# First layer's cross attention: one TensorE step interleaves both passes, GpSimd splits the maxima, and the second pass runs fifteen steps behind the first

## The reference, cut to what matters

```python
# q = x, k = v = ctx_2048, each (32, 64, 256); 8 heads split the 64 rows of a sequence
qk = jnp.einsum('bhdq,bhdl->bhql', qh, kh) * scale      # dq = 8, Lq = Lk = 256
sm = jax.nn.softmax(qk, axis=-1)
ret = jnp.einsum('bhql,bhdl->bhdq', sm, vh)
x = _layernorm(x + gamma * ret)
```

## Time and profile before

| | us |
|---|---|
| median of 3 runs | 1250.38 (1249.96 to 1255.8) |
| profiled execution | 1244.66 |
| its span in the trace | 1242.6 |
| cross attention within the span, about | 163 to 428 |
| PE, DVE, ACT, POOL busy in the span | 1103.5, 800.7, 585.0, 454.7 |
| DMA, sums and products (line 779), issue to landing, the page's median | 3.0 |

### The profile page before, as it was taken

How to read it: one execution, slowest core, us unless ns; L and a number is a source line. 1 busy time by engine, 2 the same in 40 slices (tenths; PEclk the granted TensorE clock), 3 DMA queues, 4 the chain that set the end, 5 groups by cost and what they waited for, 6 DMA issues and landing times. The chain is left out here.

```text
span 1242.6 us, 20732 instructions
## 1 busy us (share of the span) xinstructions
PE 1103.5 (89%) x7356; PEld 652.4 (53%) x7356; DVE 800.7 (64%) x1547; ACT 585.0 (47%) x1209; POOL 454.7 (37%) x692
## 2 busy tenths in 40 slices
PE   6888769998998599999878999869997999999997
PEld 3566535454554245777433555647775343545455
DVE  4899886888886142333576668647885456465555
ACT  2666506766767331343376555348773422121110
POOL 6999851555534245333235346431111000000001
PEclk9999978999999799999999999989997999999999
DMA  6964354655662112453503000020000000000000
GB/s 219 309 192 143 94 131 106 147 139 142 149 143 73 47 56 97 125 170 120 174 1 135 1 1 1 1 69 2 2 2 5 21 1 0 9 9 9 8 9 26
DMA packets 75354, 95.90 MB, mean 77 GB/s; under 512 B 12883, under 2 KB 62189, under 8 KB 74573
## 3 DMA queue, kind: packets, MB, share of 16 engines
q1 hardware_dynamic: 70835, 84.92, 24.1%
q0 software_dynamic: 3408, 9.34, 2.1%
q10 hardware_dynamic: 1010, 0.31, 0.1%
HBM read 57.47 MB, written 31.27 MB: 71 GB/s over the span
## 5 line engine op out<-in xcount | busy, mean ns | idle before, releaser
L918 ACT ACTIVATE a_late<-a_qkv 128x512 f32<-128x512 f32 x128 | 77.3, 604 | 59.3 <-PE a_qkv L995 59.3
L2654 POOL TENSOR_SCALAR f_rstd<-f_mv 128x1 f32<-128x1 f32 x16 | 3.8, 239 | 266.5 <-DVE f_mv L2793 266.4
L866 DVE TENSOR_REDUCE b_nm<-a_s 128x4 f32<-128x1024 f32 x64 | 78.0, 1219 | 30.8 <-PE a_s L964 30.8
L2738 DVE TENSOR_TENSOR f_prod<-f_sg,f_kept 128x512 f32<-128x512 f32 (+1 forms) x48 | 33.2, 692 | 96.4 <-ACT f_kept L2683 93.5
L2863 PE MATMUL fps_h<-residT,w_f_w 128*128 128x512 f32 x176 | 82.4, 608 | 2.5 <-DVE f_inner L2775 2.5
L866 DVE TENSOR_REDUCE b_nm<-a_pt 128x4 f32<-128x1024 f32 x64 | 76.7, 1199 | 2.3 <-PE a_pt L964 2.3
L918 ACT ACTIVATE a_late<-a_y 128x512 f32<-128x512 f32 x128 | 77.0, 602 | 0.0
L2677 ACT ACTIVATE f_sg<-fps_h 128x512 f32<-128x512 f32 (+1 forms) x24 | 14.3, 596 | 125.2 <-PE fps_h L2882 108.3
L1010 PE MATMUL a_o<-a_late,b_vt 128*32 128x256 f32 x1024 | 69.2, 389 | 0.0
L1320 POOL DMA_INDIRECT routed<-c_out,c_target x39 | 37.4, 959 | 67.2 <-ACT c_out L1401 66.9
L1974 DVE SCALAR_TENSOR_TENSOR d_acc<-d_pad,d_cw,d_acc 128x512 f32<-128x512 f32 x72 | 58.4, 815 | 4.9 <-ACT d_acc L1880 3.2
(11 more groups left out here) (428 smaller groups left out, 2896.9 us busy)
## 6 DMA issues: line engine op xcount, KB each, us to landing
kparts<-a_rest SPq DMA_DIRECT2D x48, 192.0 KB, 3.8
a_rest<-a_rest SPq DMA_DIRECT2D x64, 128.0 KB, 3.0
xrows<-in_c_fill SPq DMA_DIRECT2D x13, 387.0 KB, 4.5
c_xrow<-xrows SPq DMA_DIRECT2D x39, 129.0 KB, 2.1
c_back<-routed SPq DMA_DIRECT2D x16, 256.0 KB, 3.6
a_front<-kparts SPq DMA_DIRECT2D x12, 288.0 KB
a_front<-qparts SPq DMA_DIRECT2D x36, 96.0 KB
qparts<-b_xp SPq DMA_DIRECT2D x48, 64.0 KB, 2.8
```

The lines of the kernel that those rows point to most:

```text
L866: dve.tensor_reduce(nm[s % 2][:, 4 * n:4 * n + 4].rearrange("p (g h) -> p g h", h=2), s1[step % 2][:], AX.X, ALU.max, negate=True).then_in ...
L918: act.activation(pr[g % 8][:], s2[g % 2][:], ACT.Exp, scale=SCALE).then_inc(s2_out, 1)
L2738: dve.tensor_tensor(prod[n % 2][at], sg[n % 2][at], up, ALU.mult).then_inc(prod_done, 1)
```

## The change

Five things are changed, all in `cross_attention`.

1. PE's step is written in another order. Before: first pass (4 matmuls), both heads of the second pass (2 + 2), and in every other step all 8 value matmuls. Now: half of the values (4 matmuls, one `lh`) in every step, second pass of head 2j, first pass, second pass of head 2j + 1.
2. ACT's step has `products_out` first, then the exponential of head 2j, then `maxima_out`, then that of head 2j + 1.
3. `split_maxima` leaves DVE for POOL, at the end of POOL's round.
4. `T_AT` is 3 instead of 2.
5. `LAG` is `STEPS + 7` = 15 instead of 14.

```diff
-    LAG = STEPS + 6
+    LAG = STEPS + 7
...
-    T_AT, REC_AT, STATS_AT, TURN_AT = 2, 4, 6, 4
+    T_AT, REC_AT, STATS_AT, TURN_AT = 3, 4, 6, 4
...
             if live(s - 3):
                 sums(s - 3)
                 norm(s - 3)
+            if live(s):
+                split_maxima(s)
...
                 if step >= AHEAD_MAX:
                     maxima(dve, step)
-                if n == STEPS - 1:
-                    split_maxima(s)
...
-            if n == T_AT and live(s - 1):
-                maxima_out(s - 1)
-            x, j = divmod(step - LAG, STEPS)
-            if live(x):
-                exps(x, 2 * j)
             y, at = divmod(step - LAG - 4, STEPS)
             for half in range(2):
                 if at == 4 * half + 2 and live(y):
                     products_out(y, half)
+            x, j = divmod(step - LAG, STEPS)
+            if live(x):
+                exps(x, 2 * j)
+            if n == T_AT and live(s - 1):
+                maxima_out(s - 1)
             if live(x):
                 exps(x, 2 * j + 1)
...
+        def values(x, q, lh):
+            if lh == 0:
+                pe.wait_ge(s2_out, G * x + 4 * q + 4)
...
+            for j in range(4):
+                g = 4 * q + j
+                ins = pe.matmul(o_ps[32 * j:32 * j + 32, q % 2, :], vt[x % 2][:, lh, g, :], pr[g % 8][:, lh, :],
+                                start=(lh == 0), stop=(lh == KD - 1))
+            if lh == KD - 1:
+                ins.then_inc(pv_done, 1)
...
+            y, at = divmod(step - LAG - 3, STEPS)
+            if live(y):
+                values(y, at // KD, at % KD)
+            x, j = divmod(step - LAG, STEPS)
+            if live(x):
+                second_pass(x, 2 * j)
             if live(s) and step >= AHEAD:
                 first_pass(pe, step)
             if n == T_AT and live(s - 1):
                 turn_maxima(s - 1)
-            x, j = divmod(step - LAG, STEPS)
             if live(x):
-                second_pass(x, j)
-            y, at = divmod(step - LAG - 3, STEPS)
-            if live(y) and at % 2 == 0:
-                values(y, at // 2)
+                second_pass(x, 2 * j + 1)
```

More of the change, by code:

```diff
@@ L849, in norm, with split_maxima @@
             gp.tensor_scalar(x[:, 3, :], x[:, 2, :], mv[v][:, 0:1], rstd[v][:], ALU.subtract, ALU.mult).then_inc(rn_done, 1)
+        def split_maxima(s):
+            m, left, full = mp[s % 2], nrest[s % 2], nm[s % 2]
+            gp.wait_ge(s1_out, STEPS * (s + 1))
+            if s >= 2:
+                gp.wait_ge(mp_turned, s - 1)
+            gp.tensor_copy(m[:, 0, :], full[:]).then_inc(m_steps, 1)
+            gp.wait_ge(m_steps, 4 * s + 1)
+            gp.tensor_tensor(left[:], full[:], m[:, 0, :], ALU.subtract).then_inc(m_steps, 1)
+            gp.wait_ge(m_steps, 4 * s + 2)
+            gp.tensor_copy(m[:, 1, :], left[:]).then_inc(m_steps, 1)
+            gp.wait_ge(m_steps, 4 * s + 3)
+            gp.tensor_tensor(left[:], left[:], m[:, 1, :], ALU.subtract).then_inc(m_steps, 1)
+            gp.wait_ge(m_steps, 4 * s + 4)
+            gp.tensor_copy(m[:, 2, :], left[:]).then_inc(m_split, 1)
         gp.wait_ge(const, 16)
@@ L873, in vector @@
     def vector(dve):
[L874 to L887, removed]
         def inverse(t):
@@ L982, in turn_maxima, with second_pass @@
             pe.transpose(trb[0:96, :], mp[t % 2][:].rearrange("p a n -> p (a n)"), k.identb[:]).then_inc(mp_turned, 1)
-        def second_pass(x, j):
-            if x == 0 and j == 0:
+        def second_pass(x, g):
+            if x == 0 and g == 0:
                 pe.wait_ge(free.qk_out, TILES)
@@ L988, in second_pass @@
                 pe.wait_ge(free.y_out, TILES)
-            if j == 0:
+            if g == 0:
                 pe.wait_ge(m_placed[x % 2], 16 * (x // 2 + 1))
[L991 to L1006, removed]
-            for lh in range(KD):
[L1008 to L1012, removed]
+            if G * x + g >= 2:
+                pe.wait_ge(s2_out, G * x + g - 1)
+            for lh in range(KD):
+                ins = pe.matmul(s2[g % 2][:, lh, :], ks[x % 3][0:ROWS + 3, g, lh * P:(lh + 1) * P],
+                                qs[x % 3][0:ROWS + 3, g, :], start=True, stop=True)
+            ins.then_inc(s2_full, 1)
+        def values(x, q, lh):
+            if lh == 0:
+                pe.wait_ge(s2_out, G * x + 4 * q + 4)
+                if x == 0 and q == 0:
+                    pe.wait_ge(free.o_out, TILES)
+                if q == 0:
+                    pe.wait_ge(vt_done, 2 * x + 2)
+                if q % 2 == 0 and 2 * x + q // 2 > 0:
+                    pe.wait_ge(o_out, 2 * x + q // 2)
+            for j in range(4):
[4 more added lines that the diff above has]
+                ins.then_inc(pv_done, 1)
         def turn(t):
```

## The result

The changed kernel takes 1373.59 us in the median of 4 runs (1369.7 to 1385.26), where the kernel before took 1250.6 beside it: a ratio of 1.0989, 95% interval 1.091 to 1.1068. The profiled execution went from 1244.66 to 1377.46, its span from 1242.6 to 1375.4. The forecast was 1223.5, and its range ended at 1238. Where an experiment's runs spread, its ratio leaves out those that took over 1.5% more than the fastest of the same kernel (four of e6's eleven, one of e12's five), while medians and ranges are of all runs.

A forecast was written before the change was run, and what follows sets the result against it. It took PE and ACT waiting for each other as the bound in cross attention. Savings of 21.3 (steady phase), 1.0 (start) and 4.6 (end) made 26.9 us, so 1250.38 - 26.9 = 1223.5 us, range 1212 to 1238.

The forecast's parts named there:

- Start: Cross attention before step 23: step 23 comes about 1 us earlier, between 2 lost and 3 gained.
- Steady phase, PE: PE's reordered work in steady cross attention: a tile falls from 14.37 to 12.73 us, saving 1.64, without waits.
- PE's step: One new PE step in steady cross attention: 0.57 + 0.22 + 0.44 + 0.32 = 1.55 us.
- rival B: PE's transitions cost nothing: step 1.31 us, DVE then the bound, total 1213 us; chance 0.06.
- Steady phase: Cross attention from 203 to 390 us: 13 tiles at 1.64 saved each, 21.3 us in all.
- Rival A: GpSimd or the maxima's DMA late, PE waiting up to 0.6 a tile: 8 us given back, 1231; chance 0.20.
- POOL's split: Split of the maxima on POOL behind norm: 1.6 us in all, ending at 5.5, wanted at 6.6, no PE wait.
- End: From step 127's first pass to the last values: 25.8 becomes 21.1 us; 4.6 of the 4.7 saved is kept.
- Sum: Total saving 26.9 us: profiled execution from 1244.66 to 1217.8, median 1223.5 us.
- C: Rival: the wait just moves, PE still stands for ACT at the same total; 1250, at best 1246; chance 0.06.
- D: Rival: products' DMA lands late, DVE stands 2.6 us a tile and PE behind it; to 1257; chance 0.06.

The follow-up runs named there:

- e6: Changed kernel with tile 0's values in whole blocks, halves from tile 1 on, no added work: median 1233.41 us (1221.59 to 1259.15), ratio 0.9845.
- e12: e9 with SyncE sending the maxima before the first half of the next load: 1242.5 us, ratio 0.9877.
- e3: Changed kernel with all eight value matmuls together in every other step, the two second-pass heads still apart: 1236.71 us, ratio 0.9872.
- e4: Kernel before with half of the value matmuls in every step instead of all in every other: 1389.18 us, ratio 1.1101.
- e9: Changed kernel with 32 more bf16 matmuls on 128 rows before its first second pass: 1223.42 us in a single run.
- e13: Same kernel as e9, timed in five runs: median 1224.35 us (1221.62 to 1232.59), ratio 0.9772.
- e2: Changed kernel with PE's step in the order of before; split on GpSimd, lag of 15 and ScalarE's order stay: 1244.76 us, ratio 0.9923.
- e5: Changed kernel with 8 more fp32 matmuls on 128 rows before its first second pass: 1229.49 us, ratio 0.9838.
- e11: e5 with the split of the maxima back on VectorE: 1232.95 us, ratio 0.9814.
- e8: Changed kernel with tile 0's values in whole blocks and the last of four value groups whole in each later tile: 1239.57 us, ratio 0.9877.
- e7: Kernel before with value halves in every step from tile 1 on, whole blocks in tile 0: 1278.21 us, ratio 1.0228.

## Why the prediction was wrong, step by step

**The step that failed is in the part "Start".** It said that PE is at the lower clock there and that things, "carried on at these rates", come out 1 us earlier at step 23. For that I took the rise of the clock near 196 over from the trace of before as if it were given by the time. It was a consequence of the order: the halves kept it from coming (e3 and e4), and all 104 steps of the steady phase and most of the end were then at the lower level. With it failed the price of every group in "Steady phase, PE": 0.57, 0.22, 0.44 and 0.32 were read at 1.00 and measured 1.02, 0.40, 0.85 and 0.56 at 0.50. No rival covered this; the clock came up as 1.00 in the steady stretch and as the lower one at the start, and nowhere as something that could stay. Yet the earlier trace rows held the hint, the pair of 0.58 at 186.56 against 0.38 in the earlier trace rows, and I used it for the price of a few steps only, not as a question: what must happen for this to become 0.38 again?

At the lower level the new step is 2.83, 2.90 with the turns, against 1.797 before: over 104 steps that is 114.3 of the 117.1 us.

**The rest is tested by e9 and e13, which have the clock and 32 matmuls more.** Point by point:

*PE's step.* Forecast 1.55 of 0.57, 0.22, 0.44, 0.32. PE in e9, a step without a turn:

```profile
264.27 0.64 PE L1013 MATMUL a_o<-a_late,b_vt 128*32 128x256 f32 x8
264.85 0.39 PE L998 MATMUL a_qkv<-b_qs,b_ks 75*128 75x256 bf16 x2
265.07 0.60 PE L965 MATMUL a_s<-a_middle 72*128 72x256 bf16 x4
265.51 0.38 PE L998 MATMUL a_y<-b_qs,b_ks 75*128 75x256 bf16 x2
265.83 0.64 PE L1013 MATMUL a_o<-a_late,b_vt 128*32 128x256 f32 x8
```

From start to start 0.58, 0.22, 0.44 and 0.32, in all 1.56. Right; so rival B, free transitions, is out.

*Steady phase.* Its step 23 is at 202.40 and its step 127 at

```profile
369.14 0.60 PE L965 MATMUL a_pt<-a_front 72*128 72x256 bf16 x4
```

so 166.7 us, 12.83 a tile against 12.73 forecast: 20.1 saved where 21.3 were expected. An undisturbed tile takes 12.70; the difference is mostly PE's wait for the DMA of the maxima, 1.4 us in all, at most 0.8 at once. The same 104 steps, at 1.00 throughout, show what each piece is worth in one execution each: 186.85 before, 180.64 in e2 (everything but PE's order), 173.24 in e3 (the two heads apart) and 166.7 in e9 (halves too). Rival A's second half is there, in small: the room of 5.15 us for the landing wasn't always enough.

*POOL's split.* Forecast 1.6, by rows 7 and 8. POOL in e5:

```profile
255.61 0.20 POOL L857 CAST b_mp<-b_nm 128x32 bf16<-128x32 f32 x1
255.89 0.24 POOL L859 TENSOR_TENSOR b_nrest<-b_nm,b_mp 128x32 f32<-128x32 f32 x1
256.20 0.21 POOL L861 CAST b_mp<-b_nrest 128x32 bf16<-128x32 f32 x1
256.49 0.25 POOL L863 TENSOR_TENSOR b_nrest<-b_nrest,b_mp 128x32 f32<-128x32 f32 x1
256.80 0.21 POOL L865 CAST b_mp<-b_nrest 128x32 bf16<-128x32 f32 x1
```

1.40 from first start to last end, and PE never waited for it. On DVE before, the five ran from 263.48 to the end of the last:

```profile
264.48 0.21 DVE L887 CAST b_mp<-b_nrest 128x32 bf16<-128x32 f32 x1
```

That is 1.21, so POOL takes 1.2 times as long. The Trainium skill's GPSIMD Engine Reference (introduction) has the Vector engine "roughly 2×" faster; for these narrow operations the trace does not bear that out, and the measured rows decide.

*Start.* 203.27 became 202.40, 0.9 saved for 1.0 forecast, which is luck, since the reason is another: the added matmuls cost some 5 us and the earlier clock gave them back. In e6, with no work added, step 23 comes at 201.07, 2.2 earlier than before and inside the range of the forecast.

*End.* In e9 the last values end at 391.97, 22.8 after step 127's first pass, for 21.1 forecast and 25.8 before: 3.0 saved, not 4.6. Steps without a copy of products or a turn take 1.21 to 1.25, not 1.11, and those with a copy 1.4 to 1.6: PE waits 0.2 to 0.4 for that copy before the values, and ACT is late behind it.

*Sum.* 20.1 + 0.9 + 3.0 = 24.0 in the stage and 21.2 in the profiled execution (1244.66 to 1223.42), while the medians beside each other are 30.3 apart (1254.68 and 1224.35); 26.9 was forecast. The sum of the forecast was thus near for a kernel that has the clock, and e6's three fastest runs (1221.59 to 1224.10) come out there without added work. The changed kernel hasn't the clock.

*Rivals C and D.* C, the wait only moves: not so, in e9 no matmul waits for ACT between steps 23 and 127. D, the products' DMA: in e5 and e9 DVE waited for it not once before step 127, and three times behind it, 4.6 to 7.0 us each, as the kernel before does too (3.8 to 9.4). Right to give it little, and the loss came by a way that stood in none of the four.

## What to carry to other kernels

When a reordering touches PE and the stage has PE at the lower clock in its start, the rise of the clock belongs to the prediction: ask what PE did before it rose in the trace, and whether the new order still does that. A steady tile at 1.00 says nothing about how it got there. And a schedule that can run at two speeds needs a way back up: e6, e11 and e12 fell in mid-stage and stayed down for 48 to 75 us, each behind a wait of 1.3 to 1.4 us for a DMA, and e6's upper runs are some 30 us above its fastest. e8, with a whole block in each tile, came back after 24.

## What the runs showed of the hardware that I had not expected

- In the changed kernel the granted clock stayed at 0.50 for 365 us (171 to 536), and from 190 to 536 PE had no idle time. In the Trainium skill, "TensorE: Matmul & The Clock Gate", Part 1, activity releases the throttled state; here busy time without a gap was not enough, and the measurement decides.
- At the lower level 32 bf16 matmuls on 72 rows did not raise the clock and 32 on 128 rows did; 8 in fp32 on 72 rows did not and 8 on 128 rows did. Only these four were tried, in one place of one kernel.
- The value matmuls, on 128 rows, in blocks of 8 every other step came ahead of a rise (before, e2, e3, e6, e7), in blocks of 4 every step they did not as long as first passes stood between them; and yet the higher level, once reached, held in the second order for 208 us (188.5 to 396.7 in e9).
